# Decoder kernel, second stage: conv tap and two evictions moved from ScalarE to VectorE, and TensorE's output products dealt around the small projections

## The reference

```python
# layer 0, cross attention (scores over the context, values are the normalised x)
query = ctx @ Wq.T + bq ; key = ctx @ Wk.T + bk            # 512 x 128 each
att = softmax(query @ key.T) ; x = x + att-weighted sum of layernorm(x)
# layer 1, state-space part, the half of it that needs ctx only
xp = pad(in_proj_w @ ctx)                                  # 512 channels, 3 zeros in front
u = silu(conv4(xp) + conv_b)                               # 4 taps per channel
dbl = x_proj_w @ u ; dt_lo, Bm, Cm = split(dbl)            # 48 rows
dt = dt_proj_w @ dt_lo + dt_proj_b ; delta = softplus(dt)
# kept for the later scan: delta, delta * u, D * u, Bm, Cm
```

## Time and profile before

| | |
|---|---|
| median of three runs | 2496.56 us (2494.91 to 2501.55) |
| the profiled execution | 2496.56 us, its span 2494.4 us |
| `stage_context` in the span | about 931 to 1179 us |
| busy over the whole span | PE 87%, DVE 70%, POOL 43%, ACT 38% |
| mean granted clock of TensorE | 0.943 of full speed |

### The profile page before, as it was taken

The page is one execution under the profiler, slowest core; times in us unless marked ns, Lnnn a source line. Parts: engine busy times, 40 slices in busy tenths (PEclk is TensorE's granted clock), DMA queues, the critical chain, the costliest instruction groups (busy, mean ns, idle before and its releaser), DMA issues. The chain is left out here.

```text
span 2494.4 us, 25433 instructions
## 1 busy us (share of the span) xinstructions
PE 2168.2 (87%) x7344; PEld 1118.2 (45%) x7344; DVE 1734.7 (70%) x2952; ACT 952.5 (38%) x1812; POOL 1082.3 (43%) x805
## 2 busy tenths in 40 slices
PE   6998999899899978773799898999589999999848
PEld 3554554455454533331555646565233433434224
DVE  1787688868768887674688888889636464554454
ACT  1433343334334425553554646565113232332310
POOL 2454343334435414664689898999400000000033
PEclk9999999999999989896899999999789999999979
DMA  7000000000000013455752636453222121221021
GB/s 254 18 18 20 17 19 22 19 20 22 17 18 22 20 38 132 170 191 195 272 190 98 210 115 213 149 201 107 93 60 59 35 54 48 51 51 38 14 105 51
DMA packets 95549, 214.79 MB, mean 86 GB/s; under 512 B 15824, under 2 KB 33104, under 8 KB 93024
## 3 DMA queue, kind: packets, MB, share of 16 engines
q1 hardware_dynamic: 77184, 156.18, 19.4%
q10 hardware_dynamic: 17760, 57.42, 6.6%
q0 software_dynamic: 512, 0.13, 0.0%
HBM read 146.30 MB, written 42.07 MB: 76 GB/s over the span
## 5 line engine op out<-in xcount | busy, mean ns | idle before, releaser
L706 POOL TENSOR_SCALAR a_prob<-a_prob,a_rsum 128x256 f32<-128x256 f32 x256 | 146.9, 593 | 466.7 <-DVE a_rsum L634 466.4
L1344 DVE TENSOR_TENSOR_SCAN s_state<-s_decay,s_state 128x512 f32<-128x512 f32 x256 | 304.5, 1209 | 12.3 <-ACT s_decay L1286 11.9
L1300 POOL TENSOR_TENSOR s_state<-s_b_rows,s_delta_u 128x1024 f32<-128x1024 f32 x128 | 303.6, 2385 | 16.7 <-DMA s_b_rows<-scan_bc 14.3
L1462 PE MATMUL c_bank<-c_xn_parts,c_w_parts 128*128 128x512 f32 (+1 forms) x1056 | 273.8, 410 | 1.5 <-DVE c_xn_parts L1538 1.4
L1286 ACT ACTIVATE s_decay<-s_delta,s_a 128x512 f32<-128x512 f32 x256 | 173.4, 689 | 223.7 <-DVE s_state L1344 223.1
L2008 POOL DMA_DIRECT2D d_qs<-d_neg_t x16 | 8.2, 513 | 514.0 <-DVE d_neg_t L1939 514.0
L1462 PEld LDWEIGHTS c_bank<-c_xn_parts,c_w_parts 128*128 128x128 f32 (+1 forms) x1056 | 199.4, 190 | 63.1 <-issue 14.5
L438 PE MATMUL a_bank<-a_xn_t,a_wq 128*128 128x512 f32 x512 | 227.2, 592 | 0.0
L549 ACT ACTIVATE a_prob<-a_score,a_neg_m 128x256 f32<-128x256 f32 x256 | 117.8, 476 | 278.5 <-DVE a_neg_m L629 278.3
L521 PE MATMUL a_bank<-a_wo,a_out_t 128*128 128x512 f32 x512 | 222.3, 592 | 0.0
L1860 ACT ACTIVATE d_prob_t<-d_score 128x512 f32<-128x512 f32 x256 | 138.9, 595 | 192.2 <-PE d_score L1743 191.2
(11 more groups left out here) (196 smaller groups left out, 3725.9 us busy)
## 6 DMA issues: line engine op xcount, KB each, us to landing
s_b_rows<-scan_bc SPq DMA_DIRECT2D x64, 512.0 KB, 3.7
c_w_parts<-ffn_weights_hi ACTq DMA_DIRECT2D x39, 512.0 KB, 3.8
c_w_parts<-ffn_weights_lo ACTq DMA_DIRECT2D x39, 512.0 KB, 4.7
f_idx<-in_idx SPq DMA_DIRECT2D x64, 130.0 KB, 2.1
ffn_weights<-f_picks SPq DMA_DIRECT2D x64, 130.0 KB, 1.8
r_factor<-in_factors SPq DMA_DIRECT2D x8, 1024.0 KB, 8.0
d_qs<-d_hi SPq DMA_DIRECT2D x128, 64.0 KB, 2.0
d_ks<-d_hi SPq DMA_DIRECT2D x128, 64.0 KB, 2.0
```

The source lines that it names most:

```text
L1300: pool.tensor_tensor(self.state[:, s], row.broadcast_to([P, 2, T]), self.delta_u[:, h % 2], ALU.mult) \
L1344: dve.tensor_tensor_scan(self.state[:, s, e, :], self.decay[u % 2][:], self.state[:, s, e, :], 0.0, ALU.mult, ALU.add).then_inc(self.scann ...
L1462: mm = nc.tensor.matmul(banks[b][0:width[o], :], w_parts[:, n % SLOTS, w, at:at + width[o]], xn_parts[:, x_, k, :], start=((k, w, x_) == t ...
```

## The change

- Conv tap 0 moves from ACT (`nc.scalar.activation` with a scale, the function `tap`) to DVE (`tensor_scalar`), so that DVE does sixteen conv instructions and not twelve. `conv_step` counts all sixteen.
- Of the four evictions of the normalised x, those of `k` = 0 and 2 move from ACT to DVE, behind tap 0.
- The eviction of `dt` with its bias moves from ACT to DVE, ahead of the four instructions of line 1083.
- On DVE the adds of output tiles 1 to 3 move behind those, ahead of the next layer norm; only tile 0 is added before.
- On PE `weigh` 0 stays in its place, `weigh` 1 comes between `dbl` and `dt`, and `weigh` 2 and 3 come after `dt`.
- ACT no longer waits for `zeroed`.

```diff
 (PE)
-                for tt in range(TT):
-                    weigh(i, tt)
+                weigh(i, 0)
                 pe.wait_ge(w_rest_in, 16 * 4)
                 pe.wait_ge(u_ready, (i + 1) * ET + 1)
...
                 mm.then_inc(m_ring.full[b], 1)
+                weigh(i, 1)
                 pe.wait_ge(m_ring.free[b], turn + 1)
                 for et in range(ET):
...
+                weigh(i, 2)
+                weigh(i, 3)
 (ACT)
-                tap(i, (0, 1))
                 pad(i, (2, 3))
-                tap(i, (2, 3))
-                for step, out in [(("xn", k), xn_t[:, k, :]) for k in range(KD)] + \
+                for step, out in [(("xn", k), xn_t[:, k, :]) for k in (1, 3)] + \
...
-                for et in range(ET):
-                    b, turn = m_ring.at(("dt", et), i)
-                    act.wait_ge(m_ring.full[b], turn)
-                    nc.scalar.activation(dt[:, et, :], m_banks[b][:], ACT.Identity, bias=cols[:, et, DC + 1:DC + 2]) \
-                        .then_inc(m_ring.free[b], 1)
 (DVE)
-                for tap in range(1, DC):
+                for tap in range(DC):
                     for et in range(ET):
-                        if tap == 1:
-                            dve.wait_ge(first_tap, i * ET + et + 1)
+                        src = padded[:, et, tap:tap + T]
+                        if tap == 0:
+                            b, turn = m_ring.at(("x", et), i)
+                            dve.wait_ge(m_ring.free[b], turn + 1)
+                            ins = nc.vector.tensor_scalar(conv[:, et, :], src, cols[:, et, 0:1], None, ALU.mult)
                         else:
...
+                    if tap == 0:
+                        for k in (0, 2):
+                            b, turn = ring.at(("xn", k), i)
+                            dve.wait_ge(ring.full[b], turn)
+                            nc.vector.tensor_copy(xn_t[:, k, :], banks[b][:]).then_inc(ring.free[b], 1)
-                add(i, (0, 1, 2))
                 b, turn = m_ring.at(("dbl",), i)
                 dve.wait_ge(m_ring.full[b], turn)
                 dve.wait_ge(stored, i * STORES + 1)
                 nc.vector.tensor_copy(dbl[:], m_banks[b][0:DR + 2 * DS, :]).then_inc(m_ring.free[b], 1)
-                add(i, (3,))
+                add(i, (0,))
+                for et in range(ET):
+                    b, turn = m_ring.at(("dt", et), i)
+                    dve.wait_ge(m_ring.full[b], turn)
+                    nc.vector.tensor_scalar(dt[:, et, :], m_banks[b][:], cols[:, et, DC + 1:DC + 2], None, ALU.add) \
+                        .then_inc(m_ring.free[b], 1)
...
                                                    op0=ALU.mult, op1=ALU.min).then_inc(neg_abs, 1)
+                add(i, (1, 2, 3))
                 if more:
                     norm_vector(nc, dve, norm, x, i + 1)
```

More of the change, by code:

```diff
@@ L846, in stage_context @@
     zeroed = core.sem("m_zeroed")
-    first_tap = core.sem("m_first_tap")
     conv_step = core.sem("m_conv_step")
-    TAPS = ET * (DC - 1)
     u_ready = core.sem("m_u_ready")
@@ L980, in pad @@
                     act.wait_ge(m_ring.full[b], turn)
-                    act.wait_ge(conv_step, i * TAPS + 1)
+                    act.wait_ge(conv_step, i * (ET * DC) + 1)
                     nc.scalar.copy(padded[:, et, DC - 1:], m_banks[b][:]).then_inc(m_ring.free[b], 1)
[L984 to L991, removed]
             act.wait_ge(w_in, 16 * 6)
-            act.wait_ge(zeroed, 1)
             with act.Fori(0, B) as i:
@@ L1019, in _ @@
                 for et in range(ET):
-                    act.wait_ge(conv_step, i * TAPS + (DC - 2) * ET + et + 2)
+                    act.wait_ge(conv_step, i * (ET * DC) + (DC - 1) * ET + et + 2)
                     nc.scalar.activation(u[:, et, :], conv[:, et, :], ACT.Silu, bias=cols[:, et, DC:DC + 1]) \
                         .then_inc(u_ready, 1)
-                for et in range(ET):
-                    b, turn = m_ring.at(("dt", et), i)
-                    act.wait_ge(m_ring.full[b], turn)
-                    nc.scalar.activation(dt[:, et, :], m_banks[b][:], ACT.Identity, bias=cols[:, et, DC + 1:DC + 2]) \
-                        .then_inc(m_ring.free[b], 1)
                 for et in range(ET):
@@ L1064, in one_pass @@
                 dve.wait_ge(u_ready, i * ET + 1)
-                for tap in range(1, DC):
+                for tap in range(DC):
                     for et in range(ET):
-                        if tap == 1:
-                            dve.wait_ge(first_tap, i * ET + et + 1)
-                        else:
[L1070 to L1073, removed]
-                add(i, (0, 1, 2))
+                        src = padded[:, et, tap:tap + T]
[3 more added lines that the diff above has]
+                            ins = nc.vector.tensor_scalar(conv[:, et, :], src, cols[:, et, 0:1], None, ALU.mult)
+                        else:
+                            dve.wait_ge(conv_step, i * (ET * DC) + (tap - 1) * ET + et + 2)
+                            ins = nc.vector.scalar_tensor_tensor(
+                                out=conv[:, et, :], in0=src, scalar=cols[:, et, tap:tap + 1],
+                                in1=conv[:, et, :], op0=ALU.mult, op1=ALU.add)
+                        ins.then_inc(conv_step, 1)
+                    if tap == 0:
[3 more added lines that the diff above has]
+                            nc.vector.tensor_copy(xn_t[:, k, :], banks[b][:]).then_inc(ring.free[b], 1)
                 b, turn = m_ring.at(("dbl",), i)
```

## The result

The changed kernel takes 2530.03 us in the median of four runs (2526.53 to 2531.70), beside 2496.40 us for the kernel before: 1.0132 of its time, 95% interval 1.0117 to 1.0145, 33.6 us slower. The forecast was 2542 us, in a range of 2503 to 2555.

A forecast was written before the change was run, and what follows sets the result against it. No engine is full in `stage_context`; a loop of hand-overs between engines bounds it. Later `dt` starts and DVE's wait behind `dt` add 13.9, 10.1, 12.8 and 8.3 us, together 45, to 2496.56: 2542 us, range 2503 to 2555.

The forecast's parts named there:

- the conv: Last tap ends 32.2 us after the first row-maximum in passes 1 to 3; in pass 0 at 976.7, not 973.4.
- The end of the pass on DVE: `dt` start to the next row-maximum takes 25.2 us, not 19.0: 6.1 us more; in pass 3, 1.3 more.
- my signs: Profile after: at least two taps of about 5 us per pass, PE idle 5 us or more ahead of `dbl`.
- PE: `dbl` starts 0.9 us behind the last tap, `dt` 6.9 us after `dbl`, plus 2.5 us for the low clock.
- By pass: Passes 0 to 3 of the stage take 13.9, 10.1, 12.8 and 8.3 us more, together 45 us.
- Rival A: Conv not delayed, only the new order costs: 5.8 us more, 2502 us; chance 0.14.
- Rival B: Work added to DVE simply adds: 5.6 us a pass, 22 us, 2519 us; chance 0.12.
- Rival C: Faster: `u` is always ready when `weigh(i, 0)` ends; -14.0 us, 2483 us; chance 0.07.
- ACT's relief at nothing: Taking 4 taps, 2 copies and 4 `dt` off ACT was costed at nothing, ACT being idle half the time.

The follow-up runs named there:

- stats_first: The changed kernel with the next layer norm's statistics moved on DVE ahead of the adds of output tiles 2 and 3; 2519.3 us, ratio 1.0094.
- factor_late: The changed kernel with POOL's two factor additions moved behind `D * u`; 2508.3 us, ratio 1.0049.
- all_four: The changed kernel with factor additions behind `D * u`, layer-norm statistics ahead of tiles 2 and 3, conv part undone, ACT's first roundings behind silu; 2486.9 us.
- after_taps: all_four with POOL's factor additions back at their old place, behind a wait for the last tap; 2475.8 us, ratio 0.9919.
- conv_back: The changed kernel with its conv part undone (tap 0 and all evictions of the normalised x on ACT again); 2516.0 us, ratio 1.0089.
- dt_back: The changed kernel with the `dt` eviction on ACT again; 2536.4 us, ratio 1.0157.
- conv_only: The kernel before with only the conv part of the change (tap 0 and two evictions of the normalised x on DVE); 2502.8 us, ratio 1.0031.

## Why the prediction was right

The place, the sign and the mechanism were right; the size was 45 us where the stage shows 37.6 and the runs 33.6. Of the 7.4 us too many in the stage, 7.2 are in one term, the conv, 1.8 us in each of the four passes; the errors of the others nearly cancel.

- *The end of the pass on DVE.* I had 25.2 us from `dt` to the next maximum in place of 19.0. It is 24.91 in passes 0 and 1 and 26.60 in pass 2, where PE made the last two output tiles in 8.83 us and not 7.13 with a low clock. Shown by stats_first, which takes 3.6 us of it away in passes 0 and 1 and 5.3 in pass 2. The last pass: 11.4 us from `dt` to the softplus lines, I had 11.2.
- *The conv.* I had the last tap at M + 32.2 in passes 1 to 3; it is 30.4. The step that was mis-sized is where the old taps begin: M + 10.7, not 12.1, so that eight were done ahead of the first factor and not seven. The rest went as counted: two factors, two weight pieces. In pass 0 I had 28.5 us (976.7 less 948.16), it is 26.7: between the second factor and the weight pieces POOL waited for ACT, and two taps ran free. That one `tensor_scalar` with one SBUF source waits for POOL was only my reading; the 4.72 us above show it, and factor_late, where the old taps of pass 0 begin 8.5 us behind the maximum and not 12.8. Of my signs, two did not hold in pass 0: it has only one DVE instruction of about 5 us (the second wait is 3.81 us), and PE waits 4.91 us for `u`, not 5 or more.
- *PE.* I had 9.4 us from `dbl` to `dt` with 2.5 us for the clock. It is 8.9, 9.0, 8.8 and 9.6 in the four passes. In all_four and after_taps it is 7.19 in every pass, with a granted clock of 1.00 in pass 0 of all_four (960 to 975 us), so the clock costs 1.6 to 2.4 us a pass here.
- *By pass*, `dt` and end together: 11.2, 7.6, 11.9 and 6.8 us, where I had 13.9, 10.1, 12.8 and 8.3.
- *Rival A* (only the order costs, 2502 us; its terms add up to 5.6 us, not 5.8): conv_back is that kernel in effect, and takes 2516 us, with 16.7 us in the stage. Its forecast lacked ACT's stand for a weight piece (`dbl` comes 3.6 us behind the last tap in passes 1 to 3, not 0.9) and the low clock of PE while the last output tiles are made (`dt` to the next maximum 28.3 and 26.6 us in passes 1 and 2, not 25.2).
- *Rival B* (added work adds): dt_back and conv_only speak against it. The Trainium skill's page Perfetto Trace Analysis, Optimizing Scalar/DVE Operations, says that VectorE and GpSimd share an SBUF read port; the trace agrees (5.00 us for a tap beside a factor). By the same section VectorE is faster where it has a faster mode, and giving work away may pay if it is saturated. DVE was busy 155.85 of the stage's 231.48 us before and 193.95 of 269.07 after, waits for POOL counted in, so it was not saturated, and the conv part still cost 14 us. Whether it ran in a faster mode, no run shows.
- *Rival C* (`u` in time makes it faster): false for the change, but the conditions that I gave for it, taps over by M + 21 in pass 1 and by 963 in pass 0, are met in after_taps (M + 17.5 and 962.4), together with other edits, and that kernel is faster.
- *ACT's relief at nothing*: dt_back agrees for the four `dt`. For the taps and copies no run separates ACT's relief from DVE's added work.

The whole runs' 33.6 us are 4 below the stage's 37.6: 2.9 us, because the profiled execution of the changed kernel was that much above its median, and the rest in the other stages, which differ by more than that from one profile to the next.

## What to carry to other kernels

A late result costs what the work between it and its consumer does not cover. When an order is changed so that a wait goes away, look up in the trace what had stood in that wait, and compare when the producer is done with when its result is now needed. Here either half of the change alone cost the stage 4 and 17 us, and the two together 38. In a queue that is served in order, put work that is ready ahead of the instruction that waits for another engine. And look at where GpSimd's long instructions stand: moving the same additions away from VectorE instructions with SBUF sources alone gave 22 us in one kernel (after to factor_late) and 11 us in another (all_four to after_taps).

## What the runs showed of the hardware

A VectorE instruction with one float32 SBUF source and an SBUF result can wait for a GpSimd instruction in full (4.72 us in the changed kernel, where four such of the layer norm run 0.46 us apart), as one with two sources does (5.00 us). In pass 1 of conv_only it was the other way round by the profile: four taps ran ahead of an addition that had begun and that took 2.8 us longer for the two; what decides which engine goes first, no run tells. Alternating with GpSimd's instructions of 128x512 (the attention weights), the `tensor_scalar` comes every 0.83 us (pass 0 of the changed kernel) and a tap every 1.10 us (pass 1 of the kernel before). TensorE's granted clock was 0.81 and then 0.73 in the mean, so partly 1.2 GHz, in two stretches of conv_back in which PE was busy all the time, 7 us and more after it had waited for 2.15 us, with 1.00 in between; I had counted on a low clock only right behind a long wait. Where such a stretch falls moves from pass to pass: the last two output tiles took 7.13 us in pass 0 of the changed kernel and 8.83 in pass 2. No run shows why.
